# A sixteen-head attention with a folded feed-forward: where two turned layers, one variance and a few small steps stand at the change-over

## The reference

```python
x = x + attention(ctx, ctx, layernorm(x))      # 16 heads; softmax over the heads (axis=1)
x = x + ffn(layernorm(x))
# ffn: h = x; for each of three blocks:
#     y = linear(h); y = layernorm(y)*g + b; y = gelu(y); y = linear(y); h = y + h
# linear: weights dequantised from int32 with a scale per group of 16, plus a rank-32 term and a bias
```

## Time and profile before

| | us |
|---|---|
| median of 3 runs | 358.87 |
| lowest, highest | 358.61, 361.41 |
| the profiled execution | 358.84 |
| its span, first to last instruction | 356.9 |

### The profile page before, as it was taken

How to read it: one execution, slowest core, us unless ns; L and a number is a source line. 1 busy time by engine, 2 the same in 40 slices (tenths; PEclk the granted TensorE clock), 3 DMA queues, 4 the chain that set the end, 5 groups by cost and what they waited for, 6 DMA issues and landing times.

```text
span 356.9 us, 13104 instructions
## 1 busy us (share of the span) xinstructions
PE 340.4 (95%) x4808; PEld 254.6 (71%) x4808; DVE 327.8 (92%) x822; ACT 289.0 (81%) x588; POOL 267.3 (75%) x288
## 2 busy tenths in 40 slices
PE   7979999999999999999999989978999999999995
PEld 6546567667767766766766767856888888888874
DVE  7889999999999999999999999878999999988774
ACT  4688888888878878887887868488989999999982
POOL 6448888877987987897799998878777778774231
PEclk9999999999999999999999999999999999999999
DMA  7978557648646744854753400000110001110112
GB/s 204 239 243 266 172 163 217 209 129 245 195 132 202 222 157 150 264 167 140 222 162 109 151 2 2 2 1 3 30 32 29 29 29 41 50 32 29 42 48 89
DMA packets 54530, 43.29 MB, mean 121 GB/s; under 512 B 4624, under 2 KB 48608, under 8 KB 54496
## 3 DMA queue, kind: packets, MB, share of 16 engines
q1 hardware_dynamic: 53920, 42.31, 39.4%
q10 hardware_dynamic: 576, 0.53, 0.5%
HBM read 26.05 MB, written 16.78 MB: 120 GB/s over the span
## 4 chain that ended last, share of the span: by engine, by line
PE 61%; DVE 23%; issue 6%; ACT 5%; POOL 4%; DMA 1%; DVEq 0%; ACTq 0%; POOLq 0%
PE score_ps L1687 8%; DVE zsum L856 6%; PE att_ps L1648 6%; PE score_ps L1591 6%; DVE negmax L840 5%; PE wo_ps L1427 5%; PE score_ps L1439 4%; PE score_ps L1781 3%; PE work L1463 3%; PE work L1774 3%; DVE st L886 3%; PE att_ps L1781 2%; PE work L1476 2%; PE work L1469 2%; PE score_ps L1681 2%
## 5 line engine op out<-in xcount | busy, mean ns | idle before, releaser
L527 POOL TENSOR_TENSOR probs<-probs,rz 128x1024 f32<-128x1024 f32 x64 | 136.3, 2141 | 27.3 <-DVE rz L859 27.3
L578 POOL TENSOR_TENSOR rs<-ve,minus_half 128x4 f32<-128x4 f32 (+1 forms) x47 | 55.7, 1186 | 34.7 <-DVE ve L786 24.1
L856 DVE TENSOR_REDUCE zsum<-probs 128x64 f32<-128x1024 f32 x64 | 77.3, 1208 | 2.4 <-ACT probs L1164 2.3
L1164 ACT ACTIVATE probs<-score_ps 128x1024 f32<-128x1024 f32 x64 | 65.6, 1025 | 14.5 <-PE score_ps L1591 13.9
L840 DVE TENSOR_REDUCE negmax<-score_ps 128x64 bf16<-128x1024 f32 x64 | 75.2, 1176 | 0.8 <-PE score_ps L1439 0.8
L1427 PEld LDWEIGHTS wo_ps<-wo_t,att_t 128*128 128x128 f32 x256 | 36.9, 191 | 13.4 <-issue 12.0
L1687 PEld LDWEIGHTS score_ps<-lin_t,h 128*128 128x128 f32 x304 | 36.9, 191 | 11.3 <-DVE h L939 7.1
L1648 PE MATMUL att_ps<-probs,v_diag 128*32 128x64 f32 x2048 | 43.4, 224 | 1.1 <-POOL probs L527 0.7
L1252 ACT ACTIVATE z<-score_ps,rs 128x128 f32<-128x128 f32 x152 | 43.6, 383 | 0.6 <-POOL rs L578 0.6
L1687 PE MATMUL score_ps<-lin_t,h 128*128 128x128 f32 x304 | 39.7, 278 | 1.9 <-DVE h L939 1.9
L1648 PEld LDWEIGHTS att_ps<-probs,v_diag 128*32 128x32 f32 x2048 | 32.8, 109 | 10.9 <-POOL probs L527 2.7
(11 more groups left out here) (278 smaller groups left out, 692.7 us busy)
## 6 DMA issues: line engine op xcount, KB each, us to landing
q_parts<-parts SPq DMA_DIRECT2D x15, 512.0 KB, 3.5
k_stack<-k_parts SPq DMA_DIRECT2D x30, 256.0 KB, 3.3
q_stack<-q_parts SPq DMA_DIRECT2D x60, 128.0 KB, 2.9
x_all<-in_x SPq DMA_DIRECT2D x16, 256.0 KB, 3.9
ctx_sb<-in_ctx SPq DMA_DIRECT2D x16, 256.0 KB, 3.7
k_parts<-parts SPq DMA_DIRECT2D x16, 256.0 KB, 2.9
out<-x_all SPq DMA_DIRECT2D x15, 256.0 KB, 2.3
q_parts<-parts SPq DMA_DIRECT2D x4, 128.0 KB, 2.3
```

Of the source, the lines that this page charges most:

```text
L527: nc.gpsimd.tensor_tensor(e[:, :, :, :], e[:, :, :, :], by_query.broadcast_to([P, BANDS, SEQ, ADJ]), ALU.mult).then_inc(s_probs, 1)
L578: nc.gpsimd.tensor_tensor(rs2[v][:, lo:hi], ve2[v][:, lo:hi], minus_half[:, lo:hi], ALU.pow).then_inc(p_rs[v], 1)
L856: nc.vector.tensor_reduce(zsum[q][:, :], probs[(p - 1) % 4][:, :, :, :].rearrange("p u k s -> p k u s"), AX_XY, ALU.add).then_inc(s_zsum, 1)
L1164: nc.scalar.activation(probs[p][:, :, :, :], score_ps[p % 2][:, :].rearrange("p (u s k) -> p u k s", s=ADJ, k=SEQ), ACT.Exp, scale=SCALE). ...
```

## The change

- `last_turned_layers` and `late_layers` go. Layer 3 is made by `hidden_layer` in `fourth_step_closes` (17,2), behind the second layer, after a wait for the sixteenth attention addition (`s_x2` 16), in `wo_ps`; ACT copies it (`one_layer(3, 4)`) in step 4, ahead of `turned_input`. Layer 5 is made by `output_layer` in PE's step 6, ahead of block 1's second layer, in `work0`, and copied in ACT's step 6 after block 1's Gelu; PE's step 7 waits for it. The bf16 matmul goes without a substitute.
- DVE's early step 2 goes. ACT runs four Square activations of 128x128 from PSUM, each with a summed output, ahead of Exp of pair (15,1); POOL makes the variance of the sums in one operation. The semaphore counts of `combine_input` are lower by two.
- `transpose_z(0, 1)` moves from (15,0) to (15,1) on PE; `transpose_z(1, 1)` from (17,2) to (16,3).
- The attention addition of chunk 12 moves ahead of the sum of pair (14,2) in DVE's (14,3).

```diff
@@ -51,7 +51,7 @@
 EARLY = {"PE": {1: (14, 1), 2: (15, 0)},
-         "DVE": {2: (15, 1)},
+         "DVE": {},
          "ACT": {1: (14, 1), 2: (15, 2), 4: (16, 2)},
@@ -122,6 +122,7 @@
         res_cols = sb("res_cols", [P, 2])
+        y_sq = sb("y_sq", [P, TPC])
         seed = sb("seed", [P, 2, P])
@@ -234,7 +235,6 @@
         p_xbn, p_xmv, p_xst, p_xrs = sem("p_xbn"), sem("p_xmv"), sem("p_xst"), sem("p_xrs")
-        p_ysq = sem("p_ysq")
         p_z0 = sem("p_z0_scaled")
@@ -310,7 +310,7 @@
-            home, place = {1: (att_ps, 1), 2: (att_ps, 2), 4: (wo_ps, 0), 0: (work1, 0), 3: (bank[0], 0), 5: (bank[0], 1)}[i]
+            home, place = {1: (att_ps, 1), 2: (att_ps, 2), 4: (wo_ps, 0), 0: (work1, 0), 3: (wo_ps, 0), 5: (work0, 0)}[i]
             return home[:, P * place:P * (place + 1)]
@@ -534,33 +534,25 @@
-            def token_variance(lo, count, moments, mv, st_done):
-                st, ag = st2[1][:, lo:lo + TPC, :], ag2[1][:, :, lo:lo + TPC]
-                pool.wait_ge(moments, count)
+            def token_variance(count, mv):
+                st, ag = st2[1][:, 0:TPC, :], ag2[1][:, :, 0:TPC]
+                pool.wait_ge(p_xbn, count)
                 nc.gpsimd.tensor_tensor(ag[:, 1, :], st[:, :, 2], st[:, :, 5], ALU.add)
-                if lo == 0:
-                    nc.gpsimd.tensor_tensor(ag[:, 0, :], st[:, :, 1], st[:, :, 4], ALU.add)
+                nc.gpsimd.tensor_tensor(ag[:, 0, :], st[:, :, 1], st[:, :, 4], ALU.add)
                 nc.gpsimd.tensor_tensor(ag[:, 2, :], st[:, :, 1], st[:, :, 4], ALU.subtract).then_inc(mv, 1)
                 pool.wait_ge(mv, 2 * count - 1)
-                if lo == 0:
-                    nc.gpsimd.tensor_scalar(ag[:, 1, :], ag[:, 1, :], 4.0 / D, 4.0 * EPS, ALU.mult, ALU.add)
-                    nc.gpsimd.tensor_scalar(nm2[:, :], ag[:, 0, :], -0.5, None, ALU.mult)
-                    nc.gpsimd.tensor_tensor(ag[:, 3, :], ag[:, 2, :], ag[:, 2, :], ALU.mult).then_inc(mv, 1)
-                else:
-                    nc.gpsimd.tensor_scalar(ag[:, 1, :], ag[:, 1, :], 1.0 / D, EPS, ALU.mult, ALU.add)
-                    nc.gpsimd.tensor_scalar(ag[:, 0, :], ag[:, 2, :], 0.25, None, ALU.mult).then_inc(mv, 1)
-                    pool.wait_ge(mv, 2 * count)
-                    nc.gpsimd.tensor_tensor(ag[:, 3, :], ag[:, 2, :], ag[:, 0, :], ALU.mult).then_inc(p_ysq, 1)
-                    pool.wait_ge(p_ysq, 1)
+                nc.gpsimd.tensor_scalar(ag[:, 1, :], ag[:, 1, :], 4.0 / D, 4.0 * EPS, ALU.mult, ALU.add)
+                nc.gpsimd.tensor_scalar(nm2[:, :], ag[:, 0, :], -0.5, None, ALU.mult)
+                nc.gpsimd.tensor_tensor(ag[:, 3, :], ag[:, 2, :], ag[:, 2, :], ALU.mult).then_inc(mv, 1)
                 pool.wait_ge(mv, 2 * count)
-                nc.gpsimd.tensor_tensor(ve2[1][:, lo:lo + TPC], ag[:, 1, :], ag[:, 3, :], ALU.add).then_inc(st_done, 1)
+                nc.gpsimd.tensor_tensor(ve2[1][:, 0:TPC], ag[:, 1, :], ag[:, 3, :], ALU.add).then_inc(p_xst, 1)
...
                     pool.wait_ge(p_nmr, t)
-                token_variance(0, t + 1, p_xbn, p_xmv, p_xst)
+                token_variance(t + 1, p_xmv)
@@ -585,7 +577,9 @@
                 if isinstance(t, int) and t == 2:
-                    token_variance(TPC, 1, p_bn[1], p_mv[1], p_st[1])
+                    pool.wait_ge(p_bn[1], 1)
+                    nc.gpsimd.tensor_scalar(ve2[1][:, TPC:2 * TPC], y_sq[:, :], 1.0 / D, EPS, ALU.mult,
+                                            ALU.add).then_inc(p_st[1], 1)
                 own = later(t)
@@ -774,6 +768,12 @@
+            def add_attention(k):
+                dve.wait_ge(s_wo, k + 1)
+                nc.vector.tensor_tensor(x_all[:, k, :, :], wo_ps[:, :].rearrange("p (t d) -> p t d", t=TPC),
+                                        x_all[:, k, :, :], ALU.add).then_inc(s_x2, 1)
@@ -801,13 +801,13 @@
                 nc.vector.tensor_tensor(ag[:, 2, :], st[:, :, 1], st[:, :, 4], ALU.subtract).then_inc(p_mv[1], 1)
-                dve.wait_ge(p_mv[1], 2 * k - 3)
+                dve.wait_ge(p_mv[1], 2 * k - 5)
                 if lo == 0:
...
                                                ALU.mult).then_inc(p_mv[1], 1)
-                dve.wait_ge(p_mv[1], 2 * k - 2)
+                dve.wait_ge(p_mv[1], 2 * k - 4)
                 nc.vector.scalar_tensor_tensor(ve2[1][:, lo:hi], ag[:, 1, :], 1.0 / D, ag[:, 3, :], ALU.mult,
@@ -847,6 +847,8 @@
                         input_stats_of(c + 3)
+                    if p == 3 and isinstance(c, int) and c == NCHUNK - 2:
+                        add_attention(c - 2)
                     mc = c - (p == 0)
@@ -857,12 +859,8 @@
                         nc.vector.reciprocal(rz[(p - 1) % 4][:, :], zsum[q][:, :]).then_inc(s_rz, 1)
-                    if p == 3 and live(c - 2):
-                        dve.wait_ge(s_wo, c - 1)
-                        nc.vector.tensor_tensor(x_all[:, c - 2, :, :],
-                                                wo_ps[:, :].rearrange("p (t d) -> p t d", t=TPC),
-                                                x_all[:, c - 2, :, :], ALU.add).then_inc(s_x2, 1)
+                    if p == 3 and live(c - 2) and not (isinstance(c, int) and c == NCHUNK - 2):
+                        add_attention(c - 2)
                     if isinstance(c, int) and (c, p) == (1, 0):
@@ -1015,12 +1013,6 @@
-            def late_layers():
-                act.wait_ge(s_lint_ps, 4)
-                nc.scalar.activation(lin_t[:, 3:6:2, :], bank[0][:, 0:2 * P].rearrange("p (l d) -> p l d", l=2),
-                                     ACT.Copy).then_inc(s_lint, 1)
@@ -1181,6 +1173,8 @@
+                if isinstance(c, int) and c == NCHUNK - 1:
+                    first_squares()
                 if live(c):
@@ -1217,8 +1211,6 @@
                     exponentials(3)
-                if isinstance(c, int) and c == NCHUNK - 1:
-                    late_layers()
                 if live(c + 3):
@@ -1243,6 +1235,14 @@
+            def first_squares():
+                act.wait_ge(p_y[1], 1)
+                for t in range(TPC):
+                    ins = nc.scalar.activation(z[1][0][:, t, :], first_layer_bank(1, 2, 0)[:, TILE * t:TILE * (t + 1)],
+                                               ACT.Square, accum_out=y_sq[:, t:t + 1])
+                ins.then_inc(p_bn[1], 1)
@@ -1285,9 +1285,9 @@
                 gelu(1, t - 3, transpose_bank(1, t, par))
+                if isinstance(t, int) and t == 6:
+                    one_layer(5, 5)
                 if live(t - 5):
-                    if isinstance(t, int) and t == FIRST_STEP:
-                        act.wait_ge(s_lint, 4)
                     if live(t - 6):
@@ -1296,6 +1296,8 @@
                     nc.scalar.activation(by_token(bank[1]), seed_rows(2), ACT.Copy).then_inc(p_seed2, 1)
+                if isinstance(t, int) and t == 4:
+                    one_layer(3, 4)
                 if live(t - 1):
@@ -1397,12 +1399,12 @@
-            def last_turned_layers():
-                pe.wait_ge(s_exp, PPC * NCHUNK - 1)
-                turned_layer(3, opens=True)
-                nc.tensor.matmul(bank[0][:, 2 * P:4 * P], ident_bf[:, :], pick_row[:, 0:2, :], start=False, stop=True,
-                                 skip_group_check=True)
-                turned_layer(5).then_inc(s_lint_ps, 1)
+            def hidden_layer():
+                pe.wait_ge(s_x2, NCHUNK)
+                turned_layer(3, opens=True).then_inc(s_lint_ps, 1)
+            def output_layer():
+                turned_layer(5, opens=True).then_inc(s_lint_ps, 1)
@@ -1582,9 +1584,6 @@
-                    if isinstance(c, int) and (c, p) == (NCHUNK - 1, 3):
-                        last_turned_layers()
@@ -1668,10 +1667,14 @@
                     early_steps("PE", c, p, step)
+                    if isinstance(c, int) and (c, p) == (NCHUNK - 1, 1):
+                        second_input()
                     if isinstance(c, int) and (c, p) == (NCHUNK - 1, 3):
...
                         fourth_step_opens()
+                    if isinstance(c, int) and (c, p) == (NCHUNK, 3):
+                        transpose_z(1, 1, transpose_bank(1, 4, 0))
                     if isinstance(c, int) and (c, p) == (NCHUNK + 1, 2):
@@ -1693,6 +1696,11 @@
+            def second_input():
+                pe.wait_ge(p_h[0], 1)
+                transpose_z(0, 1, bank[7], 1)
@@ -1715,9 +1723,9 @@
-                transpose_z(1, 1, transpose_bank(1, 4, 0))
                 transpose_z(0, 3, turned_input_bank(4), 1)
                 second_layer(1, second_layer_bank(1, 4))
+                hidden_layer()
@@ -1752,13 +1760,15 @@
-                if live(t - 1):
+                if live(t - 1) and not (isinstance(t, int) and t == 2):
                     if some(t - 1):
...
                     k = t - 7
+                    if isinstance(t, int) and t == 7:
+                        pe.wait_ge(s_lint, 5)
                     pe.wait_ge(p_h[2], k + 1)
@@ -1767,6 +1777,8 @@
```

(2 more changed lines are left out.)

## The result

The changed kernel takes 357.28 us (median of 8 runs, 357.10 to 357.56), the kernel before in the same session 358.76; the ratio is 0.9944, interval 0.992 to 0.9967. That is 1.5 us faster; the forecast was 358.3 with a range down to 357.4. The span of the profiled execution is 355.5 us against 356.9.

A forecast was written before the change was run, and what follows sets the result against it. DVE was taken to set the pace, held by POOL in steps 4 and 5, then PE after 263 us; gains of 0.1 + 0.4 = 0.5 us took 358.84 to 358.3 us, own range 358.0 to 358.7, overall 357.4 to 359.3.

The forecast's parts named there:

- Attention addition: At (14,3): PE's 0.63 us wait goes but is lost again waiting for POOL's product of (14,2); worth 0.
- ve4 hangs on POOL, ve3 + 5.9: L811 of step 4 ends 5.9 us after step 3's because POOL holds DVE; POOL also last in step 5, gaining 0.4.
- The transposes of (1,1): On PE before twelve output matmuls: Gelu starts near 230.4, not 232.20, but POOL sets step 4, so no added gain.
- Rival D: POOL isn't the gate: h and first layer of step 5 decide, L783 starts 0.8 us sooner; 358.0 us, chance 0.08.
- This side chain is worth at most 0.23 us by itself.: From 214.9 us, POOL's pow, z, last Exp, late copy and Gelu: DVE waits only 0.23 us for them.
- POOL's six operations become one: Step 2: pow ends 1.0 to 1.3 us sooner, z gains 0.15; worth 0 on the path, since DVE sets the pace.
- The squares: S = 1.6 us: Four Squares on ScalarE before Exp of (15,1) take 1.6 us, nothing overlapped, so DVE gives back all its 0.82.
- My own rule, 2.1 - S: Gain at the end of step 5's L811 is 2.1 us less the time of the four squares.
- rival A: The squares overlap and their sum is free: 0.85 to 1.1 us, gain 1.0 to 1.2; 357.7 us, chance 0.18.
- The new wait of step 4: PE's hidden layer waits for the last attention addition; L783 of step 5 could start 3.9 us after step 4's L811.
- rival E: The new wait is the gate: hidden layer, copy and first layer eat the 0.4; gain 0 to 0.1, 358.8 us, chance 0.14.
- Output layer in step 6: Two PE matmuls, 0.7 us, fill a 0.66 us Gelu wait, plus a 0.28 us ScalarE copy; worth 0, at worst 0.3 lost.

The follow-up runs named there:

- i_addition_back: The changed kernel with the attention addition of chunk 12 back behind sum and reciprocal; 357.08 us, ratio 0.9950 to the kernel before.
- b2_pool_later: The kernel before with a 128x384 memset on POOL ahead of the sum of z in step 3; 358.57 us, ratio 0.9999.
- a2_dve_held: The changed kernel with a 128x512 memset on DVE between statistics and variance of block 2 in step 4; 357.85 us, ratio 0.9983 to the kernel before.
- f_turn_back: The changed kernel with the transposes of (1,1) back at (17,2), behind the output matmuls; 357.75 us, ratio 0.9988 to the kernel before.
- d_layers_only: The kernel before with only the late layers moved (layer 3 in step 4, layer 5 in step 6); 358.22 us, ratio 0.9986.
- e_no_squares: The changed kernel with DVE's four statistics and POOL's six operations back in step 2; 358.21 us, ratio 0.9986 to the kernel before.
- g_copy_wait_later: The changed kernel with PE's wait for the copy of layer 3 moved behind block 2's first layer in step 5; 357.24 us, ratio 0.9972 to the kernel before.
- j_layers_back: The changed kernel with layers 3 and 5 and their joint copy back at (15,3); 357.94 us, ratio 0.9977 to the kernel before.
- b_pool_later: The kernel before with a 128x8 memset on POOL ahead of the sum of z in step 3; 358.64 us, ratio 0.9996.

## Why the prediction was wrong, step by step

The sum gave ve3 0.1, ve4 0.1 and ve5 0.5 us sooner; from the anchor they came 0.88, 1.78 and 1.63 us sooner.

- **Attention addition: worth 0.** Right, by the mechanism given (i_addition_back).
- **"ve4 hangs on POOL, ve3 + 5.9", and POOL is last in step 5.** This is the step that failed. I took an L786 of 1.00 us as a constant of the loop. It was the loss of a contest by 0.05 us: of the 31 L786 in the trace of before, 30 take 0.16 us. In the changed kernel L786 is level with POOL's sum and goes first, and L783 of step 5 starts at ve4 + 4.71, where the forecast has POOL let go at ve4 + 4.24. The gate there, before and after, is PE's first layer: ve5 is PE5 + 4.17 in both. My own rows said so: L783 at 237.30 took 0.17 us and started 0.34 us after POOL's chain let go. b2_pool_later shows it (ve4 0.64 us sooner, ve5 unchanged). Where the hold is put back it costs 0.45 us, only 0.19 of it through POOL (a2_dve_held).
- **The transposes of (1,1): worth 0.** Wrong with the step above. With the gate at PE's first layer, behind h, behind the second layer of block 1, they are worth 0.65 us (f_turn_back). Rival D had this gate, but with too small a move of h and a chance of 0.08.
- **"This side chain is worth at most 0.23 us by itself."** Wrong with the same step: 0.98 us. I read DVE's 0.23 us wait as all that the side chain could be worth. At ve3 that was right for the late layers (0.23 in d_layers_only). But PE's queue behind the second layer (output matmuls, the last product, first layers, transposes) moves as a whole with the first Gelu, and that queue ends in step 5.
- **POOL's six operations become one: worth 0 on the path.** The pow does end 1.20 us sooner, as forecast, and z gains 0.67 us, not 0.15. This is what the squares are worth (e_no_squares: 0.62 us at ve5).
- **The squares: S = 1.6 us.** Mis-sized: 1.01 us. The write-out exists, as assumed, but nearly all of it overlaps the next Square. My own rule, 2.1 - S, gives 1.1 us of gain in all with it, 357.7 us, the answer of rival A. That nearer number would have been luck: the rule carries the gain through DVE's sums and POOL, and neither sets step 5.
- **The new wait of step 4.** Present and named, and it is the gate, as rival E has it: PE waits 0.53 us for the copy, of which 0.18 us is the copy's own; without it PE waits for h and starts 0.18 us sooner (g_copy_wait_later). Its size was wrong in both accounts. The wait for the attention addition doesn't show in the changed kernel: it ends at 232.37, and PE begins the hidden layer at 232.77, right behind the second layer.
- **Output layer in step 6: worth 0.** Borne out: ve of step 7 follows that of step 6 by 7.43 or 7.44 us in all kernels, with it or without.
- **Parts don't add.** From before, squares give 0.00 and layers 0.34 us at ve5; squares, layers and the other small moves without the transposes of (1,1) give 0.98 (f_turn_back), all together 1.63. The last Exp needs two things that come at nearly the same time: z, behind POOL's pow, and the shift, behind PE's late layers. It starts at 14.94 before, 14.94 with the squares alone, 14.86 with the layers alone, and 14.20 with both.

What stays open: from the anchor to DVE's last instruction the profile of after is 1.88 us shorter (146.50 against 148.38), of which ve5 explains 1.63; the last 0.25 us was not followed. The medians say 1.48; ahead of the anchor, where nothing is changed, the profile of after is 0.42 us longer. The transposes of (0,1) were not tried alone, nor POOL's operations and DVE's statistics apart.

## What to carry to other kernels

An idle time of 0.23 us on the busiest engine is not the worth of the chain that ends there: follow that chain's next engine, and ask what queue moves with it. Before a long instruction is taken as a constant, look at what it waited for and at its other instances; a 128x4 operation of 1.00 us next to one of 0.16 is a contest that a shift of a few hundredths of a us decides. And where two chains meet in one instruction and are level, as POOL's pow and PE's late layers at the last Exp, cost the parts together, not one by one.

## What the runs showed of the hardware

- Summed outputs of ScalarE come as a second instruction of 0.20 to 0.22 us. With 128x128 from PSUM an ACTIVATE and its read-out follow each other every 0.25 us, and the next instruction starts 1.01 us after the first of four; behind four scaled 128x128 copies without a sum it starts after 1.00 us (219.43 to 220.43).
- Square needed no table load among the Exps; the only load at the change-over is the 1.28 us before Gelu.
- A DVE operation with two SBUF inputs that meets a POOL sum over 128x512 is held to its end within 0.03 us (before, a2_dve_held; in j_layers_back L786 ends at 230.73, POOL's sum at 230.71). Starting 0.02 us behind the sum is enough (b_pool_later, 1.04 us). It goes at full speed where it starts at the same time (after) or 0.01 us ahead (d_layers_only). The Trainium skill, SBUF — State Buffer, section on who interferes with whom, states this as an exclusive lock of a shared port pair held for a whole instruction; these traces agree, with 1.00 us against 0.16.
- Two rows don't fit such a lock, and no run explains them. In before, L800 (two SBUF inputs) takes 0.17 us at 231.91, inside POOL's pow over 128x4 (231.16 to 232.18), so this pow doesn't hold it. In a2_dve_held, L784 is recorded at 230.00 for 0.10 us inside the sum, and only the operation behind it is held.
